# Products of attention in bursts of two key tiles instead of one

## The reference, cut to what matters

```python
scores = einsum('bhqd,bhkd->bhqk', q, k) / sqrt(16)     # xa0: masked
attn   = softmax(scores, axis=-1)
ctx    = einsum('bhqk,bhkd->bhqd', attn, v)
x      = x + ctx.reshape(b, s, 256) @ W_O               # and biases
```

## Time and profile before

| what | us |
|---|---|
| median of 3 runs | 1204.88 (1201.55 to 1215.09) |
| the profiled execution, its own time | 1195.19 |
| its span, first to last instruction | 1193.5 |
| TensorE busy | 1066.2 (89%) |
| VectorE busy | 758.1 (64%) |
| ScalarE busy | 612.6 (51%) |
| GpSimd busy | 222.2 (19%) |
| mean granted TensorE clock | 0.942 |

### The profile page before, as it was taken

How to read it: one execution, slowest core, us unless ns; L and a number is a source line. 1 busy time by engine, 2 the same in 40 slices (tenths; PEclk the granted TensorE clock), 3 DMA queues, 4 the chain that set the end, 5 groups by cost and what they waited for, 6 DMA issues and landing times. The chain is left out here.

```text
span 1193.5 us, 17937 instructions
## 1 busy us (share of the span) xinstructions
PE 1066.2 (89%) x5834; PEld 540.2 (45%) x5834; DVE 758.1 (64%) x1850; ACT 612.6 (51%) x1305; POOL 222.2 (19%) x360
## 2 busy tenths in 40 slices
PE   7989999999898999999859999996989999998380
PEld 4533333333454334444636666664633444436260
DVE  4777777876578898886542222124688988856632
ACT  2236666666432777777412333321337877783250
POOL 2000000000210314324222222202001112021255
PEclk9979999999998999999969999998979999999695
DMA  8954433330079454532750401003964333302064
GB/s 291 324 148 113 122 77 74 87 72 2 1 243 286 92 132 108 134 108 64 269 189 26 169 27 34 25 17 134 301 225 105 91 75 82 69 15 71 25 175 145
DMA packets 72922, 141.74 MB, mean 119 GB/s; under 512 B 9148, under 2 KB 26176, under 8 KB 71424
## 3 DMA queue, kind: packets, MB, share of 16 engines
q1 hardware_dynamic: 68752, 130.36, 37.1%
q0 software_dynamic: 4080, 10.23, 3.1%
HBM read 86.30 MB, written 52.17 MB: 116 GB/s over the span
## 5 line engine op out<-in xcount | busy, mean ns | idle before, releaser
L960 ACT ACTIVATE r<-ps 128x512 f32<-128x512 f32 x768 | 417.9, 599 | 185.0 <-PE ps L1074 184.2
L411 DVE TENSOR_REDUCE m<-ps 128x1 f32<-128x512 f32 x512 | 320.8, 683 | 47.0 <-PE ps L1043 47.0
L1074 PE MATMUL ps<-stacks 50*128 50x512 f32 x768 | 284.9, 461 | 7.9 <-DMA stacks<-mT 4.6
L1043 PE MATMUL ps<-stacks 48*128 48x512 f32 x720 | 286.4, 475 | 3.7 <-DVE r L488 3.0
L1083 PE MATMUL ps<-r 128*32 128x512 f32 x1536 | 208.0, 614 | 1.5 <-ACT r L960 1.5
L1074 PEld LDWEIGHTS ps<-stacks 50*128 50x128 f32 x768 | 121.1, 189 | 181.9 <-ACT r L960 126.6
L407 DVE CUSTOM_DVE_ANT_0 r<-ps,r 128x512 bf16<-128x512 f32 x256 | 165.9, 688 | 52.2 <-PE ps L1043 51.6
L1043 PEld LDWEIGHTS ps<-stacks 48*128 48x128 f32 x720 | 116.7, 192 | 24.1 <-DVE m L411 14.3
L886 POOL CAST mparts<-m 128x16 fp32r<-128x16 f32 x48 | 9.9, 206 | 550.1 <-DVE m L411 316.5
L614 ACT ACTIVATE r<-ps,cols 128x512 fp32r<-128x512 f32 x48 | 33.0, 688 | 115.6 <-PE ps L675 100.8
L675 PE MATMUL ps<-r,w 128*128 128x512 f32 x192 | 90.5, 609 | 0.5 <-issue 0.5
(11 more groups left out here) (152 smaller groups left out, 1115.8 us busy)
## 6 DMA issues: line engine op xcount, KB each, us to landing
stacks<-q_parts SPq DMA_DIRECT2D x96, 192.0 KB, 3.6
stacks<-k_parts SPq DMA_DIRECT2D x96, 192.0 KB, 4.4
k_parts<-r SPq DMA_DIRECT2D x24, 512.0 KB, 3.4
q_parts<-r SPq DMA_DIRECT2D x24, 512.0 KB, 4.4
r<-in_w SPq DMA_DIRECT2D x16, 512.0 KB, 3.6
r<-in_w SPq DMA_DIRECT2D x8, 1024.0 KB, 14.4
k_parts<-r SPq DMA_DIRECT2D x24, 256.0 KB, 4.0
q_parts<-r SPq DMA_DIRECT2D x24, 256.0 KB, 4.1
```

The costliest lines, as they stand in the source:

```text
L411: ins = dve.tensor_reduce(out, mem.ps[:, bank, :], AX.X, ALU.max)
L960: act.activation(mem.probs[:, u // HG, u % HG, :], ps[:, ST + unit_of(b, g, u) % DEEP, :], ACT.Exp, scale=SCALE).then_inc(a.p_exp.sem, 1)
L1043: pe.matmul(ps[:, led_bank(n), :], stack_of(mem.qst[g], h, ROWS)[:, t * P:(t + 1) * P], stack_of(mem.kst[g], h, ROWS), start=True, stop=Tr ...
L1074: pe.matmul(ps[:, ST + N % DEEP, :], stack_of(mem.kst[g], h, KROWS)[:, kt * P:(kt + 1) * P], stack_of(mem.qst[g], h, KROWS), start=not a.m ...
```

## The change

It touches the loop of the attentions alone:

- `products` takes a range of key tiles. Bursts of two tiles (`TOGETHER` = 2) stand where `at` is a multiple of 8 and at `at` = 0: behind units 10 (tiles 0 and 1) and 2 of the next group (tiles 2 and 3), with the mask 11 and 3. The last group of the last batch keeps bursts of one tile.
- The turn of a group's products moves from unit 12 (masked 13) to 14, and VectorE's division with it.
- The two turns for the projection move from units 1 and 4 of group 1 (masked 1 and 5) to unit 4 of groups 0 and 1 (masked 5).
- The projected tiles come two at a time at unit 4 (masked 5) of groups 2 and 3, where before the first of each two stood at unit 1.
- The turn of the mask moves from unit 11 to 12; the second call into the next stage from 14 to 15.
- The maxima's own transpose keeps its units (8, masked 9).

```diff
--- before.py
+++ after.py
@@ -766,10 +766,11 @@
 ST, SB = 0, DEEP
 OB = 2 * DEEP
 MISC = OB + 1
-MASK_STEPS = ((2, 11), (3, 11))
+MASK_STEPS = ((2, 12), (3, 12))
+TOGETHER = 2
 KEY_TILES = 2
 MASK_ROUNDS = T // KEY_TILES
-NEXT_STAGE = ((3, 8), (3, 14))
+NEXT_STAGE = ((3, 8), (3, 15))
 HALF_TURN = (3, 13)
 LAST_TURN, LAST_OUT = (5, 2), (3, 4)
 AHEAD = 3
@@ -778,8 +779,8 @@
 
 
 SCHEDULE = {
-    False: (3, 8, 12, ((1, 1), (1, 4)), ((2, 1), (2, 4), (3, 1), (3, 4))),
-    True: (4, 9, 13, ((1, 1), (1, 5)), ((2, 1), (2, 5), (3, 1), (3, 5))),
+    False: (3, 8, 14, ((0, 4), (1, 4)), ((2, 4), (3, 4))),
+    True: (4, 9, 14, ((0, 5), (1, 5)), ((2, 5), (3, 5))),
 }
 
 
@@ -996,8 +997,8 @@
             G = NG * b + g
             for u in range(UNITS):
                 exps(b, g, u)
-                if a.rows is not None and not first and (g, u) in a.out_tiles[1::2]:
-                    relay(b - 1, a.out_tiles[1::2].index((g, u)))
+                if a.rows is not None and not first and (g, u) in a.out_tiles:
+                    relay(b - 1, a.out_tiles.index((g, u)))
                 if not first and (g, u) in a.out_turns:
                     oT_copy(b - 1, a.out_turns.index((g, u)))
                 if u == a.late and not (first and g == 0):
@@ -1074,15 +1075,16 @@
         pe.matmul(ps[:, ST + N % DEEP, :], stack_of(mem.kst[g], h, KROWS)[:, kt * P:(kt + 1) * P],
                   stack_of(mem.qst[g], h, KROWS), start=not a.masked, stop=True).then_inc(a.st_ps.sem, 1)
 
-    def products(G, g, kt):
-        pe.wait_ge(a.p_exp.sem, a.p_exp.at(G, HG * (kt + 1)))
-        if kt == 0:
+    def products(G, g, first, end):
+        pe.wait_ge(a.p_exp.sem, a.p_exp.at(G, HG * end))
+        if first == 0:
             pe.wait_ge(a.vg_ready.sem, a.vg_ready.at(G, 1))
             pe.wait_ge(a.ot_sb.sem, a.ot_sb.at(G))
-        for h in range(HG):
-            ins = pe.matmul(ps[h * VW:(h + 1) * VW, OB, :], mem.vg[g % 2][:, kt, h, :], mem.probs[:, kt, h, :],
-                            start=(kt == 0), stop=(kt == T - 1))
-        ins.then_inc(a.pv.sem, 1)
+        for kt in range(first, end):
+            for h in range(HG):
+                ins = pe.matmul(ps[h * VW:(h + 1) * VW, OB, :], mem.vg[g % 2][:, kt, h, :], mem.probs[:, kt, h, :],
+                                start=(kt == 0), stop=(kt == T - 1))
+            ins.then_inc(a.pv.sem, 1)
 
     def maxima(G):
         pe.wait_ge(a.cut.sem, a.cut.at(G, CUTS))
@@ -1149,9 +1151,10 @@
 
                 at = u + 1 - a.late
                 if at == 0 and not (first and g == 0):
-                    products(G - 1, (g - 1) % NG, T - 1)
-                if at > 0 and at % HG == 0:
-                    products(G, g, at // HG - 1)
+                    products(G - 1, (g - 1) % NG, T - TOGETHER, T)
+                alone = 1 if last and g == NG - 1 else TOGETHER
+                if at > 0 and at % (alone * HG) == 0:
+                    products(G, g, at // HG - alone, at // HG)
                 if not first and (g, u) in a.out_turns:
                     turn_out(b - 1, a.out_turns.index((g, u)))
                 if u == a.m_step and not (last and g == NG - 1):
@@ -1159,7 +1162,8 @@
                 if u == a.turn_step and not (first and g == 0):
                     turn(G - 1)
                 if (g, u) in a.out_tiles and not first:
-                    project_out(b - 1, a.out_tiles.index((g, u)))
+                    for t in range(2):
+                        project_out(b - 1, 2 * a.out_tiles.index((g, u)) + t)
                 if last and (g, u) == HALF_TURN:
                     turn_out(b, 0, LAST_TURN[0])
                 if a.masked and not last and (g, u) in MASK_STEPS:
@@ -1191,7 +1195,7 @@
         body(b, False, False)
     body(B - 1, False, True)
     G = B * NG - 1
-    products(G, NG - 1, T - 1)
+    products(G, NG - 1, T - 1, T)
     turn(G)
     meanwhile()
     for c in range(1, C):
@@ -1254,8 +1258,8 @@
                     maximum(dve, a, led_group, v, led_bank(unit_of(b, g, u)))
                 if u == a.turn_step + 1 and not (first and g == 0):
                     normalise(G - 1, b if g else b - 1, (g - 1) % NG, first)
-                if a.rows is None and not first and (g, u - 1) in a.out_tiles[1::2]:
-                    k = a.out_tiles[1::2].index((g, u - 1))
+                if a.rows is None and not first and (g, u - 1) in a.out_tiles:
+                    k = a.out_tiles.index((g, u - 1))
                     residual(b - 1, k)
                 if last and (g, u) in NEXT_STAGE:
                     meanwhile[NEXT_STAGE.index((g, u))]()
```

## The result

The changed kernel took **1268.13 us** (median of 4 runs, 1265.34 to 1271.3), the kernel before 1203.76 beside it: a ratio of 1.0537, 95% interval 1.05 to 1.0573. It is slower by more than the range allowed (1216 to 1260). The profiled execution took 1271.3 us, 1269.6 of them its span: 76.1 more than before, where the prediction's sum was 40. These are two single executions, and they exaggerate: that of before (1195.19) was faster than all of its four runs here, that of the changed kernel the slowest of its four. The medians are 64.4 apart.

A forecast was written before the change was run, and what follows sets the result against it. Unmasked stages were taken as bound by VectorE fed through three banks, the masked one by TensorE plus uncovered pair boundaries; +27 and +14 less 1 gave +40, 1235 us profiled, 1245 against the median, range 1216 to 1260.

The forecast's parts named there:

- the prediction's sum: Whole kernel: +27 us for two unmasked stages, +14 masked, less 1 for the first groups: +40.
- The gain of the merge: TensorE, every double burst: 1.86 us where two single ones take 2.00, 0.14 saved each.
- the masked boundaries: Masked middle batch: boundaries between unit pairs with no work on them rise from two to ten, 0.51 us each, +4.1.
- rival (d), the clock: Longer TensorE pauses bring 1.2 GHz back for long; 90 bursts take 1.86 us longer each, over 100 us; chance 0.03.
- the masked term: Masked stage: first batch +2, two middle batches +3.7 each, last +4.5; together +14 us.
- splits that pair and covers it: Masked stage: the turn, moved to 14, splits the last pair of units and covers the boundary after 15; no cost counted.
- The first batch: Masked stage, no projections: six more uncovered boundaries, 3.1 us, less 1.0 of merges: +2.
- The last: Masked stage's last batch: eight to nine more uncovered boundaries, each uncovered for longer without scores to fill them: +4.5 us.
- the unmasked term: Two stages without a mask: 3.4 + 2 x 3.2 + 3.5 = 13.3 us each, +27 together.
- (a): Rival, whole kernel faster: score tiles never short, merges and paired projections save 16 us, giving 1189; chance 0.09.
- (b): Rival, no change: unmasked gaps much smaller, masked boundaries met by ScalarE slack; within 12 us, 1193 to 1217; chance 0.06.
- (c): Rival, only one half holds: masked stage alone +14 or the other two alone +27; 1219 to 1230; chance 0.10.

The follow-up runs named there:

- Kernels 2: The kernel before with double bursts in all stages, turns and projections left where they were; 1285.72 us, ratio 1.0664.
- kernel 3: The kernel before with double bursts in the two attentions without a mask alone, nothing else moved; 1264.63 us, ratio 1.0489.
- kernel 4: The changed kernel with every transposed score of the unmasked stages computed twice into the same bank; 1293.25 us, ratio 1.0758 to the kernel before.
- kernel 6: The changed kernel with a burst's two key tiles two units apart in the unmasked stages, maxima's transpose at 6; 1236.58 us, ratio 1.0289 to the kernel before.
- kernel 10: The changed kernel with the two key tiles of each burst two units apart in all stages, masked too; 1218.72 us, ratio 1.0131 to the kernel before.
- 5: The changed kernel with only the transposed scores of units 7 to 9, 15, 0 and 1 computed twice, unmasked stages; 1284.23 us, ratio 1.068 to the kernel before.
- Kernels 1: The changed kernel with bursts of one key tile again, all other moves kept; 1222.3 us, ratio 1.013 to the kernel before.
- the eighth: The kernel before, unmasked stages with single bursts behind units 2, 7, 10, 15, turn at 13, quotients behind 15; masked stage untouched; 1192.42 us, ratio 0.9903.

## Why the prediction was right and wrong

**Right: the direction and its cause.** VectorE behind three banks, not TensorE's cycles, sets the unmasked stages. The double burst was to be 1.86 long (1.86 from its start to the next score), a group 12.15 (two of 5.99 are 11.98), VectorE's gap 1.17 (1.11 and 1.12), a half group with a turned tile 6.41 (6.40), with two projected tiles 7.43 (7.38), a middle batch 52.0 (51.5 without a slow stretch). The gain of the merge came, 0.14 a burst, and was worth nothing. The rule of the Trainium skill's page "TensorEngine Tiling (Array Packing)", section "Performance Considerations", that the prediction cited (the emptying of PSUM may become the bound) agrees with this. The same page of the Trainium skill, section "Tiling Modes", says that a change of the mode drains TensorE, and gives no size. The 0.14 fits a drain, but no run shows one by itself.

**Right as a count: the masked boundaries.** A middle batch was to have ten bare boundaries of 0.45, two of them lengthened by ScalarE's copy of a turned tile; from 210.04 to 277.75 the trace has eight of 0.45 and, behind the turned tiles, two of 0.81, where before had two.

**Wrong: rival (d), the clock.** The step that failed is "if the longer pauses of TensorE brought it back to 1.2 GHz for long, 90 bursts would take 1.86 longer each [...] Chance 0.03", set against the masked stage, which "has pauses of 0.45 and stayed at 1.00". It was treated as all or nothing. The runs show a part: 18 more stretches, each worth about 1.6 us, most of it one slow burst (3.31 for 1.92), so about 29 us in no term of the sum. Without them the changed kernel's median would lie near 1240, inside the range. The argument against was drawn from a kernel with short bursts close together; in the changed one the bursts are longer and lie further apart. Kernels 2 and 3 (falls come with the double burst), 4 (they go when TensorE is given work) and 6 and 10 (they go when the burst is split) show the cause. Which of the bursts is hit is not shown: a loop has some 30 double bursts, 5 to 8 of them were hit, and the two unmasked loops of one program differ.

**Mis-sized: the masked term.** +14 was the sum, +31.9 was measured. About 11 of it are the clock: five slow stretches, one of them twice as long as the others, at some 1.5 each (kernel 6, with the same masked loop, has middle batches of 67.7 and 69.1 with one and two), and the longer start. Some 21 remain. The middle batches grew by about 5.5 each, for 3.7. Two pieces of that are seen. The step that the turn at 14 "splits that pair and covers it" was priced at nothing: in the rows unit 14's score is followed by the turn after 0.50 (208.22 to 208.72), and the next mask comes 0.42 after unit 15's (209.28 to 209.70), where an unsplit pair has steps of 0.34 and 0.33. And the quotients, now one unit later, had no term here: they end at 211.29, the next maxima are late, the score that needs their bank starts at 212.03 and the burst 0.43 after it, some 0.2 later than TensorE alone would have had it. Together about 0.4 a group, read from these rows and not tested by itself. The first batch came out near the sum: 2.8 for 2 (kernels 4 and 5, with the same masked loop, took 65.8 where no stretch fell into it, against the 63.0 of kernel 3 with as long a start). The last grew by some 7.5, for 4.5; there the sum was an extrapolation, and no experiment takes it apart. Kernels 1 and 10 say that about 10 of the 31.9 come with the moves alone.

**Over-sized: the unmasked term.** +27 without the clock; measured 42.0 less 13 stretches of 1.6, about 21. The first batches lost less than 3.4, the middle ones 2.6 instead of 3.2. So the waits of the loops, 41 in the sum, were about 42, but that is luck: one term is 7 too small, the other 6 too large. What makes 76 of 40 is the clock, with about 29 in slow stretches and 2 in the masked start; 2 more lie outside the loops.

**The other rivals.** (a) and (b) fell with the first group of the trace. (c), one half alone, was near for kernel 3 in build but not in time.

## What to carry to other kernels

Before joining small bursts of TensorE work, compare the whole path from score to score around the joined burst (here 0.13 + 0.45 + 1.86 + 0.56 = 3.0 us) with what the banks ahead of the waiting engine hold (here 1.84 us of maxima): what is over is lost on every burst, whatever the merge saves. Splitting did better than joining in every kernel here; the eighth, with single bursts in close pairs, the quotients between two of them and the turn away from them, gave 1%, and the turn one unit later took that back. And where a change spreads TensorE's bursts further apart, put slow-clock stretches into the sum as a number of short ones with a price each, not as an event that happens or doesn't.

## What the runs showed of the hardware

The granted clock fell to half inside loops whose waits on TensorE are 0.2 to 0.8 us each, and rose again without any change in the program. All 18 falls of the changed kernel came late between two bursts: 15 when the last burst of products lay 3.3 to 5.5 us back, 3 within 0.4 us of the start of the next. The single bursts of a plain group without a mask lie less far apart (at most 1.9 us from the end of one to the next in the kernel before, 3.0 in kernel 6). But the distance is not the whole of it: most such stretches of the changed kernel passed without a fall, and so did stretches of 4 to 5 us between the single bursts of kernel 10's masked loop. Nor do the waits tell the one case from the other: the score at 967.70 had waited 0.35 and the burst at 969.67 ran slowly; the score at 981.30, at the same place of its group, had waited 0.35 too, and the burst at 983.28 ran at 2.4 GHz. The same matmuls in single bursts (kernel 6 without a mask, kernels 1, 8 and 10) kept 2.4 GHz beyond the starts, as did most of kernel 4's unmasked loops with more of them. The Trainium skill, page "TensorE: Matmul & The Clock Gate", section "Part 1: The HAM clock gate (the "warmup" mystery)", says that the throttled state is the default and that activity releases it; kernel 4, with more activity and fewer falls, agrees with that. What decides a single fall stays open.
